# A decoder layer on one core: experts in one block with the tiles, weights fetched in the last tiles, the slots' chain in quarters, and unread products on TensorE

## What is computed

```
x1 = LN(x + mixer(x))            # chunked state space mixer, its first sequence used for both
x2 = LN(x1 + cross(x1, ctx))     # 16 heads, causal, over 77 context rows
# slots ("ffn"): 16 slots per sequence, one for each of 16 experts
z  = softmax(queries(slot_query) @ keys(x2)) @ x2  # every slot over all 2048 tokens, by head
o  = slot_query + (z @ d_Wv + d_bv) @ d_Wo + d_bo  # 2 x 16 rows
h  = LN(o) * e_ln_g + e_ln_b
o  = o + (silu(h @ W1[e] + b1[e]) * silu(h @ Wg[e] + bg[e])) @ W2[e] + b2[e]   # expert e, slot e
out = LN(x2 + mha(x2, o))        # tokens attend to the 16 slots of their sequence
```

## Time and profile before

| | us |
|---|---|
| median of 3 runs | 1596.89 |
| lowest, highest | 1594.51, 1600.4 |
| profiled execution, its own time | 1594.28 |
| its span | 1592.7 |
| PE busy | 1385.3 |
| DVE busy | 806.5 |
| ACT busy | 449.5 |
| POOL busy | 234.6 |

### The profile page before, as it was taken

One profiled execution on the slowest core, in us unless ns is written; L12 is line 12 of the kernel. 1 busy time (PEld: TensorE's weight loads), 2 busy tenths in 40 slices (PEclk: granted clock), 3 DMA queues, 4 the chain that ended last, 5 costly groups with the idle time before them and its releaser, 6 DMA issues. The chain is left out here.

```text
span 1592.7 us, 26390 instructions
## 1 busy us (share of the span) xinstructions
PE 1385.3 (87%) x9892; PEld 863.5 (54%) x9892; DVE 806.5 (51%) x2195; ACT 449.5 (28%) x938; POOL 234.6 (15%) x209
## 2 busy tenths in 40 slices
PE   6899999999999999999999967866676676678996
PEld 3777777777677777777777733211111111126663
DVE  0656667677786767676767743000000000004997
ACT  2434443433244444444444421000000000001333
POOL 1111111001131212121212102000000000001221
PEclk9899999999999999999999987988888888889999
DMA  9343133212212331343111108999999999972563
GB/s 352 125 139 93 57 90 93 86 49 78 87 54 97 123 113 40 112 147 114 40 59 40 46 27 349 426 423 425 426 426 424 426 426 424 426 308 65 199 199 132
DMA packets 76041, 309.27 MB, mean 194 GB/s; under 512 B 9803, under 2 KB 14923, under 8 KB 58552
## 3 DMA queue, kind: packets, MB, share of 16 engines
q1 hardware_dynamic: 72504, 293.23, 47.8%
q10 hardware_dynamic: 2432, 14.68, 2.6%
q0 software_dynamic: 1024, 0.27, 0.1%
HBM read 274.33 MB, written 33.82 MB: 193 GB/s over the span
## 5 line engine op out<-in xcount | busy, mean ns | idle before, releaser
L1441 PE MATMUL exp_bank<-all_ring,exp_hm 128*32 128x512 f32 x976 | 148.5, 723 | 100.9 <-DMA all_ring<-in_e_W 53.3
L1477 DVE TENSOR_TENSOR exp_gu<-exp_up,exp_gate 128x512 f32<-128x512 f32 x16 | 11.1, 693 | 402.2 <-ACT exp_gate L1486 402.2
L152 PE MATMUL mix_bank<-all_ring,mxw_win 128*128 128x256 f32 x672 | 156.4, 386 | 2.1 <-POOL all_ring L1331 2.1
L1441 PEld LDWEIGHTS exp_bank<-all_ring,exp_hm 128*32 128x32 f32 x976 | 30.3, 121 | 206.5 <-DMA all_ring<-in_e_Wg 78.5
L152 PEld LDWEIGHTS mix_bank<-all_ring,mxw_win 128*128 128x128 f32 x672 | 126.4, 191 | 28.5 <-issue 9.0
L1463 PE MATMUL exp_bank<-all_ring,exp_guT 128*32 128x512 f32 x512 | 119.9, 685 | 12.5 <-DVE exp_guT L1480 12.5
L1105 POOL TENSOR_TENSOR mxw_win<-mxw_win 128x1232 f32<-128x1232 f32 x32 | 72.3, 2258 | 396.5 <-DVE mxw_win L1070 396.5
L904 PE MATMUL mix_bank<-mxw_win,att_q_w 128*128 128x128 f32 x1024 | 119.8, 275 | 0.0
L904 PEld LDWEIGHTS mix_bank<-mxw_win,att_q_w 128*128 128x128 f32 x1024 | 116.9, 192 | 0.7 <-issue 0.5
L943 PE MATMUL mix_bank<-att_o_w,mxw_win 128*128 128x512 f32 x256 | 115.6, 594 | 0.0
L222 DVE SCALAR_TENSOR_TENSOR all_ring<-all_ring,mxw_taps 128x256 f32<-128x256 f32 x192 | 84.4, 482 | 53.0 <-ACT all_ring L171 50.4
(11 more groups left out here) (273 smaller groups left out, 2264.1 us busy)
## 6 DMA issues: line engine op xcount, KB each, us to landing
all_ring<-in_e_W SPq DMA_DIRECT2D x58, 2048.0 KB, 26.2
all_ring<-in_e_Wg SPq DMA_DIRECT2D x29, 2048.0 KB, 27.5
all_ring<-in_xT SPq DMA_DIRECT2D x8, 1024.0 KB, 8.0
all_ring<-scratch_rates SPq DMA_DIRECT2D x64, 128.0 KB, 4.3
all_z<-in_x SPq DMA_DIRECT2D x16, 512.0 KB, 4.6
mxw_win<-scratch_x SPq DMA_DIRECT2D x32, 256.0 KB, 2.8
scratch_x<-crs_x SPq DMA_DIRECT2D x32, 256.0 KB, 2.0
scratch_x2T<-crs_x2T SPq DMA_DIRECT2D x32, 256.0 KB, 2.0
```

The source lines that it names most:

```text
L152: last = nc.tensor.matmul(bank[:, i * BT:(i + 1) * BT], hold["win"][:, k, m * P:(m + 1) * P], hold["xT"][b % 2][:, k, :], start=(k == 0), ...
L1441: last = nc.tensor.matmul(bank[w][q * ROWS:(q + 1) * ROWS, :], hm[u][:, k, :], weights[:, at:at + FQ], start=(k == 0), stop=False)
```

## The change

**One block.** `experts_stage` becomes `expert_parts`, a set of functions that `cross_rows` calls in the same block. The exits of crs, mix, mxw and att, which stood ahead of the experts, now stand after them, with exp's. Most buffers of tiles and experts become ranges of one tensor `all_space`, so that experts' buffers take the room of what the tiles have finished with.

**Units in the last tiles.** SP issues the extra units 0 and 1 in tile 30's step, unit 2 and the slots' rows once tile 31's values are weighed. The rows come from the host in one array, already in quarters.

**Order in the last tiles.** Tile 31's output projection comes ahead of tile 30's slot scores. Sequence 0's z is divided in tile 30 and turned in tile 31. Tile 31's slot part uses other PSUM banks and another `alpha`, so that it doesn't wait for tile 30's. The last additions to z alternate with the divisions.

**Quarters.** The product with `dwo` puts its four column quarters on four groups of 32 partitions, so that `o` is 128 x 128. The layernorm works on that, and PE averages the four quarters' statistics with a matrix `even` of 0.25 (line 1707). The turn of h is one product, and so is that of `o` after the experts.

**Unread products.** `keep_busy(pe, n)` issues n products of `ident` by `ident`, whose result nobody reads, in seven places: 50 in all.

```diff
+ def turned_bank(t): return SC[:, 3, :] if at_end(t) else TO[:]
+ def slot_bank(t): return AV if at_end(t) else SLOT
+ def alpha_of(t): return last_alpha if at_end(t) else alpha
...
@@ SP
+                if isinstance(t, int) and t == LAST - 1:
+                    slots["fetch_extra"](sp, 0)
+                    sp.wait_ge(s["q_done"], TILES)
+                    sp.wait_ge(s["x1b_done"], TILES)
+                    slots["fetch_extra"](sp, 1)
             tiles(sp, step)
+            sp.wait_ge(s["av_done"], TILES)
+            slots["fetch_rows"](sp)
+            slots["fetch_extra"](sp, 2)
             store_x2(sp, LAST, 1)
             store_x2T(sp, LAST, 1)
-            for u in range(2):
-                sp.wait_ge(x2_stored[u], 16 * TILES // 2)
-                sp.wait_ge(x2T_stored[u], 16 * TILES // 2)
+            slots["stream"](sp)
@@ PE
+                if at_end(t):
+                    project_out(pe, t)
+                    slot_scores(pe, t - 1, 1 - u)
+                    return
...
             tiles(pe, step)
+            slots["turn_tokens"](pe, 0)
+            slots["keep_busy"](pe, 8)
             turn_x2(pe, LAST, 1)
+            turn_slots(pe, LAST - 1)
             slot_scores(pe, LAST, 1)
+            weigh_tokens(pe, LAST - 1, 0)
+            slots["keep_busy"](pe, 6)
             turn_slots(pe, LAST)
             weigh_tokens(pe, LAST, 1)
+            slots["keep_busy"](pe, 10)
+            slots["turn_tokens"](pe, 1)
+            slots["multiply"](pe)
@@ ACT
+                if at_end(t):
+                    slots["take_tokens"](act, 0)
+                    scale_rows(act, t, u, half)
+                    slot_exponents(act, t - 1)
+                    return
...
             take_x2T(act, LAST, 1, TILES // 2 - 1)
+            take_slotsT(act, LAST - 1)
             slot_exponents(act, LAST)
             take_slotsT(act, LAST)
+            slots["take_tokens"](act, 1)
+            slots["activate"](act)
@@ DVE
+                if isinstance(t, int) and t == LAST - 1:
+                    slots["invert_sums"](dve, 0)
+                    for m in range(SM):
+                        slots["divide_tokens"](dve, 0, m)
+                if at_end(t):
+                    residual(dve, t, u)
+                    norm(dve, t)
+                    slot_maxima(dve, t - 1, seq(-1))
+                    slot_sums(dve, t - 1, seq(-1))
+                    return
...
+            slots["invert_sums"](dve, 1)
+            for m in range(SM):
+                add_token(dve, LAST, 1, m)
+                dve.wait_ge(s["z_added"], 2 * LAST + m + 1)
+                slots["divide_tokens"](dve, 1, m)
+            slots["normalise"](dve)
@@ POOL
+            pool.wait_ge(s["o_done"], TILES)
+            slots["constants"](pool)
+            pool.wait_ge(s["z_done"], 2 * TILES)
...
+            slots["biases"](pool)
@@ expert_parts
+    def keep_busy(pe, n):
+        for i in range(n):
+            nc.tensor.matmul(bank[2][:, 0:P], hold["ident"][:], hold["ident"][:], start=True, stop=True)
+    def multiply(pe):
...
+        for g in range(GROUPS):
+            pe.wait_ge(s["znT_done"], 3 + g // 2)
...
+        keep_busy(pe, 6)
+        pe.wait_ge(s["aoT_done"], 1)
+        for g in range(GROUPS):
+            for q in range(4):
+                last = nc.tensor.matmul(bank[5][q * ROWS:(q + 1) * ROWS, 0:P], aoT[:, g, :, :], dwo[:, g, :].rearrange("p (j q) -> p q j", q=4)[:, q, :],
+                                        start=(g == 0), stop=(g == GROUPS - 1))
+        last.then_inc(s["wo_done"], 1)
+        for i in range(2):
+            keep_busy(pe, 4)
+            pe.wait_ge(s["ln_step"], (2, 4)[i])
...
+            nc.tensor.matmul(bank[7][:, i:i + 1], even[:].rearrange("p q r -> p (q r)"), stats[:, (6, 9)[i]:(7, 10)[i]], start=True, stop=True).then_inc(s["averaged"], 1)
+        keep_busy(pe, 12)
+        pe.wait_ge(s["h_done"], 1)
+        nc.tensor.transpose(bank[6][:, 0:KC * ROWS], h, hold["ident"][:]).then_inc(s["h_turned"], 1)
+        experts(pe, lambda e, u, half: expert(pe, e, u, half))
+        nc.tensor.matmul(bank[5][:, 0:KC * ROWS], o[:], hold["ident"][:], start=True, stop=False, skip_group_check=True)
+        pe.wait_ge(s["y4_done"], 1)
+        for k in range(KC):
+            last = nc.tensor.matmul(bank[5][:, k * ROWS:(k + 1) * ROWS], y4.rearrange("r (j k) -> r k j", k=KC)[:, k, :], fold[:],
+                                    start=False, stop=True, skip_group_check=True)
+    def normalise(dve):
...
+        nc.vector.tensor_tensor(o[:], bank[5][:, 0:P], slot, ALU.add).then_inc(s["ln_step"], 1)
...
+        nc.vector.bn_aggr(stats[:, 6:8], stats[:, 0:6]).then_inc(s["ln_step"], 1)
+        dve.wait_ge(s["averaged"], 1)
+        nc.vector.tensor_tensor(off, mean, bank[7][:, 0:1], ALU.subtract).then_inc(s["ln_step"], 1)
...
+        nc.vector.scalar_tensor_tensor(spread, off, off, var, ALU.mult, ALU.add).then_inc(s["ln_step"], 1)
...
+        dve.wait_ge(s["averaged"], 2)
+        nc.vector.tensor_scalar(half, bank[7][:, 1:2], EPS, -0.5, ALU.add, ALU.mult)
```

874 lines of the change are left out of this document (459 added, 415 removed).

## The result

| | before | after |
|---|---|---|
| median of 4 runs, us | 1596.57 | 1574.74 |
| lowest, highest | 1594.51, 1600.4 | 1571.48, 1578.57 |
| profiled execution, its own time | 1594.28 | 1573.41 |
| its span | 1592.7 | 1571.8 |

The ratio is 0.9861 with a 95% interval of 0.9831 to 0.9892: 22 us less, between 17 and 27. The prediction said 1577.

The account below looks back on a forecast made before the run. Experts' weights streaming from HBM at 425 GB/s bound the kernel, so its end moves with the stream's start. 19.6 + 1.3 - 1.8 = 19.1 us less gives 1575.2, or 1577.8 by the median; it said 1577, range 1570 to 1584 (8 in 10).

Parts of the forecast that it names:

- Part 1: Last tiles: fetching the three extra units there takes 6.3 MB, 14.8 us, out of what must pass between 960 and 987.
- Part 2: Chain from tile 31's output projection to expert 0's first release: first refill at 966.5 instead of 982.92.
- Bias: Slots' chain, between `dwv` and `dwo`: takes 1.2 us.
- `dwo`: Slots' output product in four column groups of 32: 1.2 us, bounds 0.6 and 3.6, ending at 958.0 before 971.93.
- layernorm: Ahead of expert 0, in quarters of 128 columns: 6.5 us instead of 7.5, with two PE averages of 0.6 each.
- Unread products: 50 in PE's waits, 0.23 us each: overhang 1.1 us in the slot part, 0.2 elsewhere; should buy full-clock durations.
- wrong: Signs against the forecast in the profile after, among them `ident` by `ident` records ending later than their wait.
- clock half lost: Rival: clock falls at z's last turns, stays at 1.2 GHz to the first release; 8 us, 1585; chance 0.11.
- Part 4: Kernel's end: turning `o` 1.3 us less, exits ahead of the combine stage 1.8 us more, combine stage itself the same.
- Ring dry: Rival: expert 0 releases units 4 and 5 too late, DMA idles for 4 to 5 us: 1582; chance 0.05.
- Late start: Rival: something behind SP's stores or small loads holds the stream, early units buy only 4.7 us: 1591; chance 0.05.
- Slower by products at half clock: Rival: clock stays at 1.2 GHz from 926, products at 0.47 us outlast the waits, release 995: 1604; chance 0.03.

Follow-up runs that it names:

- a_late1: The changed kernel with the three early units fetched behind the last tile's stores, at about 940.6, instead of at 911.6 and 929: 1576.13 us.
- b_delay: The kernel before with six copies of [32 x 512] on DVE ahead of the layernorm's last addition: ratio 0.9989 to the kernel before.
- a_double: The changed kernel with every group of unread products twice as long: 1587.42 us, ratio 0.9942 to the kernel before.

## Why the prediction came out

**The bound was the right one, and the rate of exchange too.** The stream's length was given as 429.9 us behind 1.4 of restart; it is 430.83 from issue to use. All fourteen profiles of the table fit the rule "the later of chain and backlog, then the bytes".

**Part 1 stands, with its reason narrowed.** 14.8 us of bytes were never the gain of the early fetch; it needs to be early enough that nothing is queued at the refill, and `a_late1` shows that this is met even at 940.8. The text said so only in its last half sentence.

**Part 2, the chain, was right to 0.1 us in sum, with some luck, and to 1.0 in its terms.** Projection 926.3 to 932.4: 927.30 to 933.2, since the turn's copy was waited for. x2 at 937.7 (its terms give 937.5): 938.4. Slot scores 939.7: 939.99. Last addition 949.3: 949.73. From there the errors cancel. znT was complete at 951.6, not 952.4: the last division took 0.49 us, not 0.84. For `dwv` the text says 955.5, but its own terms give 956.1 (952.4 + 3.74); measured was 955.0, since PE begins on the first half of znT, at 951.23, before the second is copied. Bias as said. `dwo` took 2.02, where I had taken 1.2 between bounds of 0.6 and 3.6: the row of the experts' products that I leaned on has 512 columns for each load of weights, this one 128, which is the likely reason and was not tested by itself. The layernorm took 6.0 for 6.5, its two averages 0.5 to 0.7 for the 0.6 of bounds 0.2 and 1.1. Refill 966.5: 966.38. Added up without the slip it would have been 967.1.

**Unread products.** I gave them 1.3 us of overhang. Cutting two groups and moving the memsets together gave 1.1 to 1.3, so the products' share of it is smaller; it was not measured alone. One sign of "wrong" was met in small: the group of six in the slot part ran until about 0.8 us behind the moment at which its wait was over, for the 1.1 in the sum. Their worth, which I had read from three rows at either level, is 3.3 us at the refill. The clock of "clock half lost" did not come either: 1.00 in the whole chain, z's turns (949.85) included. Its 8 us were much too high a price, and even with all products gone its time, 1585, was not reached (1579.3).

**Part 4 was the weak one.** The turn of `o` gave 0.6 and not 1.3: I took half of the wait of 2.91 for half of the products, but the four that remain, whose stationary operand is read with a stride of four, take 2.05 us (L1717, from 1411.61), and the copy waits 2.15. The exits took 2.1 us more for 1.8. And two effects of the clock, which I had not in the sum, nearly undid each other: 1.6 us gained in the combine weights' products, up to 1.4 lost in the first scores. The first is no work of the change: `b_delay`, in the order of before, has 3.84 us there as well. The prediction held the clock for a matter of the chain; it decides as much at the end.

**Sum.** 19.1 was said, 20.9 measured between the profiled spans: 20.3 for 19.6 up to the fourth unit, 0.6 for 1.3, -2.1 for -1.8, and 2.1 that was not foreseen (1.6 of the combine weights' products, 0.5 of the last stage). That the 2.1 fell this way is luck. On the footing of the medians the sum gave 1577.8; the measured 1574.74 is 3.1 lower, 1.8 of it by the sum and the rest within the scatter of single executions.

**What the runs don't divide.** Of the 16.5 us by which the refill comes earlier the unread products have 3.3 and the quarters 2.6. The rest belongs to the one block and to the order in the last tiles, and no run takes one of these away by itself.

**Rivals.** Ring dry: no; the share is 1.00 over the 430 us, and the dip at 982 costs 0.65. Late start: no; the refill's issue is the start (0.00 share in the us before bytes). Slower by products at half clock: its mechanism is real, `a_double` lost 9.5 us to products that outlast their waits, but from 940 on even those run at full clock (granted 1.00), and they leave the kernel faster than before (0.9942).

## What to carry to other kernels

When a stream of bytes bounds a stage, find the two things that can start it, the chain that frees the first buffer and the bytes still queued ahead; only the later one is worth work, and shortening the other is worth next to nothing (7.1 us gave 1.1). Look at DMA's share in the us before the first refill: 1.0 means fetch earlier, 0.0 means shorten the chain, and once it is 0.0, each us of the chain is one of the end, products put in to hold the clock among them, until the chain is so short that it meets what is queued. Price such products by whole waits, not by their count, and expect a few us at the end of a kernel to come and go with the granted clock.

## What the runs showed that I had not expected

- A division (DVE, [128 x 512] by a column, in place) takes 0.49 us alone and 1.26 beside a memset on POOL, while the addition that reads PSUM and stands between two of them keeps its 0.73 to 0.75. The Trainium skill, SBUF — State Buffer, Who interferes with whom, has the two engines share a port that one of them holds for a whole instruction; the rows agree.
- The product with `dwo` takes 3.62 us as 8 records of 512 columns into 32 partitions (0.45 each), and 2.02 us as 32 records of 128 columns into four groups of 32 (0.06 each): four groups side by side give 1.8 times, not four.
- Without any unread products the granted clock in the chain is 0.83 to 0.95, not 0.50: between its falls it came back with PE's own short products alone.
- Five exits cost 3.18 us from the last addition to the first scores, the one of before 1.09, and one that clears the semaphores of all five stages 1.64.
